# Two layers of cross attention and routed experts on one core: the first column scores drawn forward, loads reordered, one split moved

## The chip, the cores and the metric

The kernel runs on one core of a Trainium2 chip. Five engines work side by side, each on its own list of instructions: TensorE (PE) multiplies matrices, VectorE (DVE), ScalarE (ACT) and GpSimd (POOL) work elementwise, and SyncE (SP) issues DMA transfers and waits. They meet only at semaphores. Times are device microseconds (us) of one launch; smaller is better.

## The reference

Two batches of 256 tokens with 128 features pass through two layers. Each layer is attention over a context of 512 tokens and a mixture of experts, each with its residual. In short:

```python
def _L0_xattn_ref(query, key, value, mask, ...):        # 16 heads of 8 features
    q, k, v = proj(query, w_q, b_q), proj(key, w_k, b_k), proj(value, w_v, b_v)
    scores = einsum('bhqd,bhkd->bhqk', q, k) / sqrt(8)
    scores = where(mask == 0, -1e9, scores)
    attn = softmax(scores, axis=-1)
    return einsum('bhqk,bhkd->bhqd', attn, v) ... @ w_out.T + b_out
x = x + _L0_xattn_ref(_layernorm(x), ctx, ctx, mask, ...)
x = x + _L0_ffn_ref(_layernorm(x), ...)                  # 16 experts, 4 chosen, and a shared one
x = x + _L1_xattn_ref(_layernorm(x), ctx, ctx, ...)      # no mask
x = x + _L1_ffn_ref(_layernorm(x), ...)                  # 8 experts, 2 chosen
```

## The kernel before

All of the kernel's order is written by hand: each engine's function lists its steps, and semaphores tie them together. The change lies in the first attention, and in the first third of the span.

**Projections.** K of a batch is one matmul into a bank. To keep single precision with bfloat16 matmuls, K and Q are split into three bfloat16 parts each. The parts are written to a scratch tensor in HBM and read back in another layout (`k_stack`, `q_stack`), in which the products of the parts lie along the contraction. For K this is `k_out(i)` and `k_in(i, heads, signal)`, for Q `q_out(i)` and `q_in(i, heads, signal)`; i counts layer and batch, so 0 and 1 are the two batches of layer 0. All of these are issued by SP, in one queue. `k_split(i, part)` on GpSimd makes the three parts of K (part 0 takes the rest, part 1 the second part, part 2 the third); only K of batch 0 is split by VectorE and ScalarE. Q is split by VectorE (`q_split`, lines 770 to 775).

**One head.** The attention of a layer runs over 32 heads (16 of each batch), one step s for each, and some steps more for the pipeline to drain. For each head there are, in this order of dependence:
- row scores: `score_rows(n, qt)`, one matmul of 128 queries by 512 keys for each half of the queries (line 342); VectorE adds the mask's bias and takes the maximum of each row (`head_max`, line 791);
- for each pair of heads (group g) GpSimd splits the maxima in three (`max_split`, lines 1459 to 1462), TensorE transposes them (`max_transpose`, line 356) and ScalarE copies them into rows 96 to 98 of `q_stack` (`max_copy`);
- column scores: `score_cols(n, kts)`, the transposed scores with the maximum subtracted by the matmul itself, in two halves, each one bias matmul (line 383) and two of 256 columns (line 387); they need the second mask, turned into a bias by VectorE (`column_bias`);
- the exponential on ScalarE (line 1247), and for four heads together the product with V (`values`, line 410).

**What sets the order.** In step s TensorE issues the row scores of head s and the column scores of head s - 5 (`LAG`), the values lag 9 steps (`PV_LAG`). A head's row scores wait until the maxima of the head before have been read out of the same bank. Row scores of head 0 wait for `first_stacked`, of head 4 for `second_stacked` and `q_stacked[0]`, of head 8 for `k_stacked[0]`, of head 16 for `k_stacked[1]` and `q_stacked[1]`. GpSimd's list `maxima(groups, extra)` runs the extra steps marked g right behind max split g. SP issues the loads in the order of its list, and a wait in it holds up all that follows: the write of batch 1's K waits for its parts (`k_parts[1]`), the write of batch 1's Q for `q_parts[1]`.

Of the kernel before, what the change touches and what calls it, by code (L numbers as in the profile page):

```python
# [23 lines left out]
H, DK = 16, 8  # L24
QT, KT = S // 128, S2 // 128
PARTS = 3
# [16 lines left out]
APART = 32  # L43
LAG = 5
BEGUN = 4
PV_LAG = LAG + HG
HEADS = B * H

# [6 lines left out]
def attention_ffn_kernel(nc, x, ctxT, mask, maskT, attn_w, cols, rows, gate_bias, ties, ident,  # L55
                         gate0, gate1, wg0, wu0, wd0, wsd0, select0, wu1, bu1, wd1, bd1, out):
    ctx = ExitStack()
    with ctx:
# [211 lines left out]
        block = ctx.enter_context(nc.Block())  # L270
        use = {}

        def banks0(b, i):


            if b == 0:
                return (0, 4, 2)[i % 3], i - 3
            return (4, 2)[i % 2], PAIRS0 + i - 2 if i >= 2 else 4 + i
# [3 lines left out]
        def _(pe):  # L282
# [43 lines left out]
            def score_rows(n, qt):  # L326

                l, b, h = n // HEADS, n % HEADS // H, n % H
                if n == 0 and qt == 0:
                    pe.wait_ge(first_stacked, 16 * (PARTS + 1))  # L330
                    pe.wait_ge(k_evacuated, 2)
                if n == HG and qt == 0:
                    pe.wait_ge(second_stacked, 16 * PARTS)
                    pe.wait_ge(q_stacked[0], 16)
                if n == 2 * HG and qt == 0:
                    pe.wait_ge(k_stacked[0], 16 * PARTS)
                if n >= H and h == 0 and qt == 0:
                    pe.wait_ge(k_stacked[l * B + b], 16 * PARTS)
                    pe.wait_ge(q_stacked[l * B + b], 16)
                if n >= 1:  # L340
                    pe.wait_ge(max_done, 2 * (n - 1) + qt + 1)
                mm(bank[:, qt, :], q_stack[0:STACK, b, h, qt * 128:(qt + 1) * 128],  # L342
                   k_stack[0:STACK, b, h, :], start=True, stop=True).then_inc(for_max, 1)
# [225 lines left out]
            def attention(l, extra):  # L569


                for s in range(HEADS + PV_LAG):
                    n, m = l * HEADS + s, l * HEADS + s - LAG
                    if l * BEGUN <= s < HEADS:
                        score_rows(n, 0)
                    if 0 <= s - LAG < HEADS:
                        score_cols(m, range(0, KT // 2))
                    if l * BEGUN <= s < HEADS:
                        score_rows(n, 1)
                    if s % MG == 1 and 0 <= (s - 3) // MG < HEADS // MG:  # L580
                        max_transpose(l * HEADS // MG + (s - 3) // MG)
                    if 0 <= s - LAG < HEADS:
                        score_cols(m, range(KT // 2, KT))
                    if s % HG == (PV_LAG + 1) % HG and s >= PV_LAG + HG:
                        o_transpose(l * B * NG + (s - PV_LAG) // HG - 1)
                    if s >= PV_LAG and (s - PV_LAG) % 2 == 0:
                        values(l * B * NG + (s - PV_LAG) // HG, (s - PV_LAG) % HG // 2)
                    for at, f in extra:
                        if at == s:
                            f()  # L590
# [127 lines left out]
        def _(dve):  # L718
# [342 lines left out]
            def column_bias():  # L1061
                dve.wait_ge(ld["mask_k"], 16)
                ts(bias_k[:, :, :], mask_k[:, :, :], 0.0, MASKED, ALU.is_equal, ALU.mult).then_inc(mask_ready, 1)

            attention(0, [
                (1, lambda: column_bias()),
                (3.5, lambda: norm_stats("a0", 1, x_sb[:, 1])),
                (5.5, lambda: normalise("a0", 1, x_sb[:, 1])),
                (8.5, lambda: xT_copy("a0", 1)),
# [109 lines left out]
        def _(act):  # L1179
# [58 lines left out]
            def exponentials(n):  # L1238
                g = n // HG
                if n == 0:  # L1240

                    act.wait_ge(mask_ready, 2)
                act.wait_ge(scores_ready, n + 1)
                if n >= 2 * HG:
                    act.wait_ge(pv_done, g - 1)
                at = 2 + 2 * (n % 2)
                act.activation(probs[:, n % (2 * HG), :], bank[:, at:at + 2, :].rearrange("p a n -> p (a n)"), ACT.Exp,  # L1247
                               scale=SCALE).then_inc(exp_done, 1)
# [24 lines left out]
            def attention(l, extra):  # L1273
                for s in range(HEADS + PV_LAG):
                    if s % MG == 1 and 0 <= (s - 3) // MG < HEADS // MG:
                        max_copy(l * HEADS // MG + (s - 3) // MG)
                    if 0 <= s - LAG < HEADS:
                        exponentials(l * HEADS + s - LAG)
                    if s % HG == (PV_LAG - 1) % HG and s >= PV_LAG:
                        o_copy(l * B * NG + (s - PV_LAG) // HG)  # L1280
                    for at, f in extra:
                        if at == s:
                            f()
# [111 lines left out]
        def _(pool):  # L1395
# [13 lines left out]
            def add_row(s, b, name):  # L1409
                r = row[:, ROW_NAMES.index(name), :].unsqueeze(1).to_broadcast([128, QT, D])  # L1410
                if s == 0:
                    pool.wait_ge(ld["row"], 16)
                    pool.wait_ge(ld["x"], 16)
                if s == 2:
                    pool.wait_ge(res_ready[2], QT * (b + 1))
                if s == 3:
                    pool.wait_ge(res_ready[3], b + 1)
                pool.tensor_tensor(res_bias[s][b][:, :, :], res[s][b], r, ALU.add).then_inc(res_bias_ready[s], 1)
# [5 lines left out]
            def k_sign(b, heads):  # L1424
                pool.memset(k_stack[MAX_ROW:ROWS_K, b, heads].bitcast(F32), TWO_MINUS_ONES).then_inc(k_signed[b], 1)

            def q_zero(b):
                pool.memset(q_stack[PAD_ROW:MAX_ROW, b].bitcast(F32), 0.0).then_inc(q_zeroed[b], 1)
                pool.wait_ge(q_zeroed[b], 1)
# [13 lines left out]
            def v_bias(i):  # L1443
                l, b = divmod(i, B)
                pool.wait_ge(v_copied[i], 1)
                pool.wait_ge(ld["row"], 16)
                v = v_heads[l][:, b * KT:(b + 1) * KT, :, 0:DK]
                bias = row[:, ROW_NAMES.index(f"bv{l}"), :].rearrange("p (h d) -> p h d", h=H)
                pool.tensor_tensor(v, v, bias.unsqueeze(1).to_broadcast([128, KT, H, DK]), ALU.add)\
                    .then_inc(v_ready[i], 1)  # L1450
# [13 lines left out]
            def k_split(i, part):  # L1464

                if part == 0:
                    pool.wait_ge(k_evacuated, i + 1)
                    pool.tensor_tensor(k_rest[i][:, :], k_full[i][:, :], k_part[i][:, 0, :], ALU.subtract)\
                        .then_inc(k_rest_ready[i], 1)
                elif part == 1:  # L1470
                    pool.wait_ge(k_rest_ready[i], 1)
                    then(pool.tensor_copy(k_part[i][:, 1, :], k_rest[i][:, :]))
                else:
                    pool.tensor_tensor(k_part[i][:, 2, :], k_rest[i][:, :], k_part[i][:, 1, :], ALU.subtract)\
                        .then_inc(k_parts[i], 1)
# [13 lines left out]
            def maxima(groups, extra):  # L1489
# [4 lines left out]
                        if at == g:  # L1494
                            f()

            k_split(1, 0)
            k_split(1, 1)
            k_split(1, 2)
            maxima(range(0, HEADS // MG), [  # L1500
                (0, lambda: v_bias(0)),
                (1, lambda: root("a0", 1)),
                (2, lambda: pool.wait_ge(max_parts, 3)),
                (2, lambda: q_zero(1)),
                (3, lambda: pool.wait_ge(max_parts, 4)),
                (3, lambda: k_sign(1, slice(0, H // 2))),
                (3, lambda: pool.wait_ge(k_signed[1], 1)),
                (4, lambda: pool.wait_ge(max_parts, 5)),
                (4, lambda: k_sign(1, slice(H // 2, H))),
                (4, lambda: pool.wait_ge(k_signed[1], 2)),  # L1510
                (5, lambda: v_bias(1)),
                (6, lambda: add_row(0, 0, "bo0")),
                (7, lambda: v_bias(2)),
                (8, lambda: v_bias(3)),
                (8, lambda: k_split(2, 0)),
# [48 lines left out]
        def _(sp):  # L1564
# [6 lines left out]
            def k_out(i):  # L1571
                sp.wait_ge(k_parts[i], 1)
                sp.dma_start(k_bounce[i][:, :, 0:S2].rearrange("a p s -> p a s"), k_part[i][:, :, :]).then_inc(k_written[i], 16)
# [23 lines left out]
            q_out(0)  # L1597
            k_in(0, slice(0, HG), first_stacked)
            q_in(0, slice(0, HG), first_stacked)
            sp.dma_start(mask_k[:, :, :], maskT.rearrange("(t p) q -> p t q", p=128)).then_inc(ld["mask_k"], 16)  # L1600
            q_in(0, slice(HG, H), q_stacked[0])
            k_in(0, slice(HG, 2 * HG), second_stacked)
            k_in(0, slice(2 * HG, H), k_stacked[0])
            k_out(1)
            k_in(1, every, k_stacked[1])
            sp.dma_start(sel_f[:, :, :], select0).then_inc(ld["sel"], 16)
# [96 lines left out]
```

## Time and profile before

| | |
|---|---|
| three runs | 297.86, 299.78, 302.04 us; median 299.78 |
| profiled execution | 295.13 us, its span 293.2 us |
| TensorE busy | 247.4 us, 84% |
| VectorE | 201.1 us, 69% |
| ScalarE | 149.8 us, 51% |
| GpSimd | 82.0 us, 28% |
| mean granted TensorE clock | 0.941 |

The span runs from the first to the last instruction. A share is the busy time over the span, so it is a mean over stages with different limits. The granted clock is 1.00 at 2.4 GHz and 0.50 at 1.2 GHz. The chain that ended last consists of TensorE for 60%, VectorE 20%, DMA 5%.

### The profile page before, as it was taken

The page shows a single profiled execution, that of the slowest core. Times are in us where ns is not written, and L with a number is a line of the kernel's source. Part 1 is how long each engine was busy: PE and PEld are TensorE (multiplying, and loading weights), DVE is VectorE, ACT ScalarE, POOL GpSimd, SP SyncE. Part 2 cuts the span into 40 slices and gives each one's busy share as a digit, 9 for nine tenths or more (in the row PEclk, how much of TensorE's full clock was granted, in tenths as well). Part 3 has the DMA queues.
Part 4 walks back from the last instruction along what each step waited for, and adds up shares of the span by engine and source line. Part 5 has one row for each costly group of instructions (what it writes and reads, how often), then busy time and mean ns, then how long its engine had stood idle before and what let it go on. Part 6 is the DMA issues. An engine that isn't in the chain of part 4 may idle for free.

```text
span 293.2 us, 5209 instructions
## 1 busy us (share of the span) xinstructions
PE 247.4 (84%) x1701; PEld 141.3 (48%) x1712; DVE 201.1 (69%) x603; ACT 149.8 (51%) x218; POOL 82.0 (28%) x225
## 2 busy tenths in 40 slices
PE   3937989899977996788898898999998889898970
PEld 1611444454443573666576434444444346555670
DVE  5828767766755844597866985767676538888854
ACT  6710466557744743441322454677666535727360
POOL 8504564265522000100300341222213103433321
PEclk9985799999999998999999857999999999999997
DMA  7388597701100068600032630500000000000000
GB/s 235 134 237 180 114 192 273 185 1 57 56 1 0 2 102 128 95 0 0 0 96 69 198 90 0 161 3 1 2 2 0 1 2 1 0 2 0 19 2 18
DMA packets 18406, 19.52 MB, mean 67 GB/s; under 512 B 1996, under 2 KB 16180, under 8 KB 18036
## 3 DMA queue, kind: packets, MB, share of 16 engines
q1 hardware_dynamic: 17804, 18.25, 25.5%
q10 hardware_dynamic: 576, 0.94, 0.9%
q8 instruction: 14, 0.23, 0.3%
q14 instruction: 12, 0.10, 0.1%
HBM read 14.98 MB, written 4.19 MB: 65 GB/s over the span
## 4 chain that ended last, share of the span: by engine, by line
PE 60%; DVE 20%; issue 8%; DMA 5%; ACT 3%; SPq 1%; POOL 1%; DVEq 1%; POOLq 0%; ACTq 0%
PE bank L410 11%; PE bank L342 8%; PE bank L387 8%; PE bank L533 5%; PE bank L564 5%; DVE row_max L794 4%; PE bank L356 4%; PE bank L383 3%; DMA k_stack<-k_bounce 3%; PE bank L498 2%; PE bank L515 2%; PE bank L499 2%; PE bank L549 2%; PE bank L535 2%; DVE early L943 2%
## 5 line engine op out<-in xcount | busy, mean ns | idle before, releaser
L1247 ACT ACTIVATE probs<-bank 128x1024 f32<-128x1024 f32 x64 | 65.4, 1024 | 33.2 <-PE bank L387 28.1
L342 PE MATMUL bank<-k_stack,q_stack 72*128 72x512 bf16 x128 | 53.7, 425 | 10.4 <-DMA q_stack<-q_bounce 4.4
L791 DVE CUSTOM_DVE_ANT_0 discard<-bank,bias_q 128x512 bf16<-128x512 f32 x64 | 42.6, 689 | 26.4 <-PE bank L342 23.6
L387 PE MATMUL bank<-q_stack,k_stack 99*128 99x256 bf16 x256 | 51.6, 287 | 1.3 <-issue 1.0
L794 DVE TENSOR_REDUCE row_max<-bank 128x1 f32<-128x512 f32 x64 | 40.9, 684 | 14.0 <-PE bank L342 13.3
L1233 ACT COPY q_stack<-bank 3x512 bf16<-3x512 bf16 x32 | 18.5, 578 | 36.4 <-PE bank L356 35.7
L410 PE MATMUL bank<-probs,v_ext 128*32 128x256 f32 x512 | 35.1, 393 | 0.8 <-ACT o_sb L1254 0.8
L387 PEld LDWEIGHTS bank<-q_stack,k_stack 99*128 99x128 bf16 x256 | 24.7, 102 | 22.1 <-issue 4.7
L1459 POOL CAST max_part<-row_max 128x4 bf16<-128x4 f32 x32 | 6.6, 207 | 93.1 <-DVE row_max L794 57.2
L342 PEld LDWEIGHTS bank<-k_stack,q_stack 72*128 72x128 bf16 x128 | 12.7, 101 | 33.3 <-DVE row_max L794 9.6
L1329 ACT ACTIVATE early<-bank,col 128x256 f32<-128x256 f32 x32 | 15.5, 563 | 18.7 <-PE bank L549 18.7
L383 PE MATMUL bank<-bias_k,idb 128*128 128x512 bf16 x53 | 20.7, 391 | 0.0
L410 PEld LDWEIGHTS bank<-probs,v_ext 128*32 128x32 f32 x512 | 13.7, 110 | 13.5 <-issue 7.0
L564 PE MATMUL bank<-experts_w,early 128*128 128x128 f32 x128 | 16.3, 281 | 2.5 <-ACT early L1329 2.5
L356 PE MATMUL bank<-idb,max_part 128*3 128x128 bf16 x128 | 13.3, 231 | 6.0 <-DVEq L760 2.1
L533 PE MATMUL bank<-experts_w,xT_f 128*128 128x512 f32 x32 | 17.4, 625 | 0.0
L564 PEld LDWEIGHTS bank<-experts_w,early 128*128 128x128 f32 x128 | 14.9, 192 | 4.0 <-DVE shared_area L996 3.1
L498 PE MATMUL bank<-xT_f,experts_w 128*128 128x256 f32 (+1 forms) x52 | 16.4, 397 | 0.0
L499 PE MATMUL bank<-xT_f,experts_w 128*128 128x256 f32 (+1 forms) x52 | 15.5, 379 | 0.0
L356 PEld LDWEIGHTS bank<-idb,max_part 128*3 128x3 bf16 x128 | 7.2, 86 | 16.2 <-issue 16.2
L515 PE MATMUL bank<-experts_w,early 128*128 128x128 f32 x96 | 13.7, 292 | 1.5 <-DVE early L945 1.4
L1305 ACT ACTIVATE early<-bank 128x512 f32<-128x512 f32 x12 | 7.2, 598 | 14.6 <-PE bank L499 14.3
(179 smaller groups left out, 380.2 us busy)
## 6 DMA issues: line engine op xcount, KB each, us to landing
k_stack<-k_bounce SPq DMA_DIRECT2D x9, 384.0 KB
q_bounce<-q_part SPq DMA_DIRECT2D x12, 192.0 KB, 2.4
q_stack<-q_bounce SPq DMA_DIRECT2D x3, 576.0 KB
k_bounce<-early SPq DMA_DIRECT2D x4, 384.0 KB, 2.6
experts_w<-in_wu SPq DMA_DIRECT2D x1, 1024.0 KB, 5.1
experts_w<-in_wg SPq DMA_DIRECT2D x1, 816.0 KB, 9.4
experts_w<-in_wu SPq DMA_DIRECT2D x1, 816.0 KB, 10.9
experts_w<-in_wd SPq DMA_DIRECT2D x1, 768.0 KB, 7.2
```

Source lines behind the costliest of these rows:

```text
L342: mm(bank[:, qt, :], q_stack[0:STACK, b, h, qt * 128:(qt + 1) * 128], k_stack[0:STACK, b, h, :], start=True, stop=True).then_inc(for_max, 1)
L356: last = pe.transpose(o[:, at:at + 128], max_part[:, g % 2, j, t, :], idb[:, :])
L383: mm(bank[:, at + kts[0] // 2, :], idb[:, :], bias_k[:, kts[0]:kts[0] + 2, :].rearrange("p t q -> p (t q)"), start=True, stop=False)
L387: last = mm(o, k_stack[:, b, h, kt * 128:(kt + 1) * 128], q_stack[:, b, h, :], start=(l == 1), stop=(l == 1 or kt == kts[-1]))
L410: last = mm(bank[VW * j:VW * (j + 1), OUT, 0:S], v_ext[l][:, b * KT + kt, h * (DK + 1):h * (DK + 1) + VW], probs[:, (g * HG + j) % (2 * HG ...
L498: mm(bank[0:m, at + j, 0:S], wg0_sb[:, t * 128:t * 128 + m], xT["f0"][b][:, :], start=True, stop=True)
L499: last = mm(bank[0:m, at + j, S:2 * S], wu0_sb[:, t * 128:t * 128 + m], xT["f0"][b][:, :], start=True, stop=True)
L533: mm(o, xT["f1"][b][:, t * 128:(t + 1) * 128], wu1_sb[:, 2 * i:2 * i + 2, :].rearrange("p e n -> p (e n)"), start=True, stop=False)
L564: last = mm(bank[:, OUT, (e * QT + t) * D:(e * QT + t + 1) * D], hid1[:, w % 2, 2 * e + half, t * 128:(t + 1) * 128], wd1_sb[:, 2 * (2 * i ...
L791: ins = dve.tensor_tensor_reduce(discard[:, qt, :], bank[:, qt, :], bias_q[:, qt, :], 1.0, LOWEST, ALU.add, ALU.max, o)
L794: ins = dve.tensor_reduce(o, bank[:, qt, :], AX.X, ALU.max)
L1247: act.activation(probs[:, n % (2 * HG), :], bank[:, at:at + 2, :].rearrange("p a n -> p (a n)"), ACT.Exp, scale=SCALE).then_inc(exp_done, 1)
```

## The change

Four edits in one. Column scores of heads 0, 1, 2 and 3 of layer 0 are issued 3, 3, 4 and 4 steps behind the row scores, in steps 3, 4, 6 and 7, instead of 5 steps behind, in steps 5 to 8; the others stay at 5, so steps 5 and 8 have none. In step 3 the transposes of the first maxima go ahead of the column scores that need them. ScalarE's exponentials follow the same steps. VectorE's column bias moves from behind head 1's maxima to behind head 2's. K and Q of heads 4 to 7 are loaded ahead of the second mask, the Q load of heads 4 to 15 becomes two, of 4 to 7 and of 8 to 15. On GpSimd the split of batch 1's K, which stood ahead of all maxima, goes behind max splits 2 and 3, and the steps that stood there go one to two groups later.

```diff
+FIRST_LAGS = (3, 3, 4, 4)
...
+        def column_step(l, m):
+            return m + (FIRST_LAGS[m] if l == 0 and m < len(FIRST_LAGS) else LAG)
+        head_of_step = [{column_step(l, m): m for m in range(HEADS)} for l in range(2)]
...
                 if n == HG and qt == 0:
-                    pe.wait_ge(second_stacked, 16 * PARTS)
-                    pe.wait_ge(q_stacked[0], 16)
+                    pe.wait_ge(second_stacked, 16 * (PARTS + 1))
                 if n == 2 * HG and qt == 0:
                     pe.wait_ge(k_stacked[0], 16 * PARTS)
+                    pe.wait_ge(q_stacked[0], 16)
...
+                    transposes = s % MG == 1 and 0 <= (s - 3) // MG < HEADS // MG
+                    at_once = columns and m == n - MG - 1
                     if l * BEGUN <= s < HEADS:
                         score_rows(n, 0)
-                    if 0 <= s - LAG < HEADS:
+                    if transposes and at_once:
+                        max_transpose(l * HEADS // MG + (s - 3) // MG)
+                    if columns:
                         score_cols(m, range(0, KT // 2))
                     if l * BEGUN <= s < HEADS:
                         score_rows(n, 1)
-                    if s % MG == 1 and 0 <= (s - 3) // MG < HEADS // MG:
+                    if transposes and not at_once:
                         max_transpose(l * HEADS // MG + (s - 3) // MG)
-                    if 0 <= s - LAG < HEADS:
+                    if columns:
                         score_cols(m, range(KT // 2, KT))
...
-                (1, lambda: column_bias()),
+                (2, lambda: column_bias()),
...
-            k_split(1, 0)
-            k_split(1, 1)
-            k_split(1, 2)
             maxima(range(0, HEADS // MG), [
-                (0, lambda: v_bias(0)),
                 (1, lambda: root("a0", 1)),
-                (2, lambda: pool.wait_ge(max_parts, 3)),
-                (2, lambda: q_zero(1)),
-                (3, lambda: pool.wait_ge(max_parts, 4)),
-                (3, lambda: k_sign(1, slice(0, H // 2))),
-                (3, lambda: pool.wait_ge(k_signed[1], 1)),
+                (2, lambda: k_split(1, 0)),
+                (2, lambda: v_bias(0)),
+                (3, lambda: k_split(1, 1)),
+                (3, lambda: k_split(1, 2)),
                 (4, lambda: pool.wait_ge(max_parts, 5)),
-                (4, lambda: k_sign(1, slice(H // 2, H))),
-                (4, lambda: pool.wait_ge(k_signed[1], 2)),
-                (5, lambda: v_bias(1)),
-                (6, lambda: add_row(0, 0, "bo0")),
+                (4, lambda: q_zero(1)),
+                (5, lambda: pool.wait_ge(max_parts, 6)),
+                (5, lambda: k_sign(1, slice(0, H // 2))),
+                (5, lambda: pool.wait_ge(k_signed[1], 1)),
+                (6, lambda: pool.wait_ge(max_parts, 7)),
+                (6, lambda: k_sign(1, slice(H // 2, H))),
+                (6, lambda: pool.wait_ge(k_signed[1], 2)),
+                (7, lambda: v_bias(1)),
+                (8, lambda: add_row(0, 0, "bo0")),
...
             k_in(0, slice(0, HG), first_stacked)
             q_in(0, slice(0, HG), first_stacked)
+            k_in(0, slice(HG, 2 * HG), second_stacked)
+            q_in(0, slice(HG, 2 * HG), second_stacked)
             sp.dma_start(mask_k[:, :, :], ...)
-            q_in(0, slice(HG, H), q_stacked[0])
-            k_in(0, slice(HG, 2 * HG), second_stacked)
             k_in(0, slice(2 * HG, H), k_stacked[0])
+            q_in(0, slice(2 * HG, H), q_stacked[0])
             k_out(1)
             k_in(1, every, k_stacked[1])
```

## Rows read from the trace of the kernel before

**Rows 1.** Busy us by stretch; behind them granted clock, DMA share, GB/s.
```profile
20.00:21.00 1.00, 0.78 (x2) 0.13 (x2) 0.14 (x1) 0.00 (x0) 0.00 (x0) 0.50 1.02 352
31.00:32.00 1.00, 1.00 (x5) 0.58 (x5) 0.29 (x2) 0.58 (x1) 0.50 (x3) 0.50 0.03 8
33.00:34.00 1.00, 1.00 (x7) 0.58 (x6) 1.00 (x4) 0.16 (x1) 1.00 (x1) 0.90 0.65 173
57.00:80.00 23.00, 22.59 (x193) 11.31 (x196) 15.54 (x51) 16.26 (x21) 12.56 (x33) 1.00 0.12 39
```

**Rows 2.** Instructions in time, TensorE: start, us, operation [idle before <-releaser].
```profile
20.22 1.03 PE L342 MATMUL bank<-k_stack,q_stack 72*128 72x512 bf16 x2 [4.37 <-DMA q_stack<-q_bounce]
...
27.26 1.03 PE L342 MATMUL bank<-k_stack,q_stack 72*128 72x512 bf16 x2 [0.68 <-DMA k_stack<-k_bounce]
...
29.93 0.62 PE L342 MATMUL bank<-k_stack,q_stack 72*128 72x512 bf16 x1
...
55.63 0.38 PE L342 MATMUL bank<-k_stack,q_stack 72*128 72x512 bf16 x1 [0.72 <-issue]
```

**Rows 3.** The same view, transfers issued by SP.
```profile
17.97 0.40 SPq L1600 DMA_DIRECT2D probs<-in_maskT  x1
...
22.08 0.50 SPq L1573 DMA_DIRECT2D k_bounce<-early  x1
31.26 2.56 SPq L1580 DMA_DIRECT2D k_stack<-k_bounce  x3
...
37.70 0.47 SPq L1614 DMA_DIRECT2D experts_w<-in_wu  x1
45.17 1.49 SPq L1586 DMA_DIRECT2D q_bounce<-q_part  x3
50.19 0.32 SPq L1592 DMA_DIRECT2D q_stack<-q_bounce  x1
```

**Rows 4.** The same view, GpSimd.
```profile
11.85 1.16 POOL L1468 TENSOR_TENSOR early<-early 128x512 f32<-128x512 f32 x1 [3.03 <-ACT early L1186]
13.07 0.61 POOL L1472 CAST early<-early 128x512 bf16<-128x512 f32 x1
13.76 1.21 POOL L1474 TENSOR_TENSOR early<-early 128x512 bf16<-128x512 f32 x1
...
25.01 1.19 POOL L1449 TENSOR_TENSOR v_ext<-v_ext,row 128x512 f32<-128x512 f32 x1
...
31.36 0.20 POOL L1459 CAST max_part<-row_max 128x4 bf16<-128x4 f32 x1 [0.94 <-DVE row_max L791]
...
32.17 0.21 POOL L1462 TENSOR_TENSOR max_part<-max_rest,max_part 128x4 bf16<-128x4 f32 x1
```

**Rows 5.** The same view, VectorE.
```profile
12.22 0.93 DVE L774 CAST q_part<-q_rest 128x256 bf16<-128x256 f32 x1
13.19 0.77 DVE L775 TENSOR_TENSOR q_part<-q_rest,q_part 128x256 bf16<-128x256 f32 x1
...
30.59 0.69 DVE L791 CUSTOM_DVE_ANT_0 discard<-bank,bias_q 128x512 bf16<-128x512 f32 x1
...
44.39 0.29 DVE L774 CAST q_part<-q_rest 128x256 bf16<-128x256 f32 x1
44.72 0.43 DVE L775 TENSOR_TENSOR q_part<-q_rest,q_part 128x256 bf16<-128x256 f32 x1
```

**Rows 6.** Time from issue to landing of transfers; the first line is the K writes' (L1573).
```profile
DMA to landing us min/median/max: 2.6/2.6/9.2
...
probs<-in_maskT SPq DMA_DIRECT2D x1, 512.0 KB, 4.8
...
experts_w<-in_wu SPq DMA_DIRECT2D x1, 816.0 KB, 10.9
...
q_bounce<-q_part SPq DMA_DIRECT2D x12, 192.0 KB, 2.4
```

**Rows 7.** The chain of waits that ended last: start, us, what.
```profile
31.61 0.43 PE bank L387 x2
```

More of the change, by code:

```diff
@@ L572, in attention @@
                 for s in range(HEADS + PV_LAG):
-                    n, m = l * HEADS + s, l * HEADS + s - LAG
+                    n, columns = l * HEADS + s, s in head_of_step[l]
+                    m = l * HEADS + head_of_step[l].get(s, 0)
+                    transposes = s % MG == 1 and 0 <= (s - 3) // MG < HEADS // MG
+                    at_once = columns and m == n - MG - 1
                     if l * BEGUN <= s < HEADS:
                         score_rows(n, 0)
-                    if 0 <= s - LAG < HEADS:
+                    if transposes and at_once:
+                        max_transpose(l * HEADS // MG + (s - 3) // MG)
+                    if columns:
                         score_cols(m, range(0, KT // 2))
@@ L1276, in attention @@
                         max_copy(l * HEADS // MG + (s - 3) // MG)
-                    if 0 <= s - LAG < HEADS:
-                        exponentials(l * HEADS + s - LAG)
+                    if s in head_of_step[l]:
+                        exponentials(l * HEADS + head_of_step[l][s])
                     if s % HG == (PV_LAG - 1) % HG and s >= PV_LAG:
```

## The prediction

> **What bounds the kernel now.** The page comes first: its TensorE share (in the table above) is the highest of all engines. The busy time by stretch then says where this change can act. From 57 to 80 us TensorE is busy 22.59 of 23.00 us at full clock [rows 1], so in the steady part of the first attention nothing is won or lost unless TensorE's work changes, and it doesn't. Before that there are holes: the engine starts the heads at 20.22 after 4.37 us without work, its granted clock is then 0.50 (1.2 GHz), and it climbs to 0.90 only in the slice 33 to 34 us, after work without a hole since 29.93 [rows 1, 2]. In between it was busy 1.00 of 1 us at 0.50. The TensorE timeline shows two later waits for loads: head 4's rows at 27.26 behind K, 0.68 us, and head 16's rows (batch 1's first head) at 55.63, after 0.72 us. Two rows matmuls per head and the order of issue say that 55.63 is head 16. It is the step that needs batch 1's K and Q in SBUF; batch 1's Q load was issued at 50.19 [rows 3], so its landing, about 5.2 us later, is what ends that wait. So batch 1's loads are already the latest thing at head 16. The last view is SP's own queue, which is where the change does most.
>
> **The parts, and what each costs.**
>
> 1. *GpSimd no longer splits batch 1's K at the start.* Before, the three splits run from 11.85 to 14.97 [rows 4], beside VectorE's last two steps of batch 0's Q split: cast 0.93 and subtract 0.77, against 0.29 and 0.43 for the same two steps at 44.39, with GpSimd idle [rows 5]. These feed the Q write that the first head waits for. Gain: 0.64 + 0.34 = 1.0 us at the first head (20.2 to 19.2). The Trainium skill ("SBUF — State Buffer", section "Who interferes with whom") says that a VectorE cast in a 2-port mode, or a VectorE operation with two SBUF inputs beside a reading GpSimd operation, excludes GpSimd and the other way round; the rows agree. The same rule speaks for no slowdown where the splits go now, because the head maxima read only one operand from SBUF.
>
> 2. *Second quarter's loads ahead of the second mask.* In SP's order 288 KB of K and 144 KB of Q (from the shapes) now stand before the mask. Before, 432 + 288 = 720 KB lay between the mask's landing (17.97 + 4.8 = 22.8) and the K that released head 4 at 27.2, which is 6.1 ns a KB [rows 2, 3, 6]. So the mask lands 432 KB later and, with everything issued 1.0 earlier, at 22.8 + 2.6 - 1.0 = 24.4. Heads 4 to 7 have landed by about 22 and never wait. The bias from the mask, moved behind head 2's maxima, is ready at about 25.1. The price of the 0.68 us wait at head 4 goes to the column scores of head 0, which could start no earlier anyway, since they want the first max copy at about 25.0.
>
> 3. *Column scores of heads 0 to 3 at lags 3, 3, 4, 4.* They fill TensorE from 25.3 on. At low clock a half of the column scores takes twice the 0.43 us of two 256-column matmuls, 0.86 (the bias matmul has as many columns as those two), and a rows matmul, again 512 columns, 0.43 [rows 7]. From 25.3: columns 0 and rows 3, then columns 1 and rows 4, reach 30.1; the clock, by what the engine did before 33 (3.2 us without a hole), has risen by then. Heads 5, 6, 7 follow at full clock, paced by VectorE's 0.69 a maximum [rows 5], the statistics and the normalising of batch 1. That puts head 5's last maximum at about 31.8 and head 7's at about 35.0. By head 9 both orders are the same. TensorE arrives at head 16 some 3 us earlier than before, at 51 to 52. If head 16's data were there, this would be the gain, 3 us.
>
> 4. *Batch 1's K split between later maxima.* This is the step that decides. On GpSimd, after head 5: one max split of 1.02 (31.36 to 32.38), first K split 1.16, V bias 1.19, max split 1.02, then the two other K splits, 0.61 and 1.21, and gaps of some 0.07 between them [rows 4]: 6.4 us. From 31.8 this ends at 38.2; head 7's maxima at 35.0 don't hold it. Before, the parts were ready at 14.97.
>
> SP waits for these parts ahead of everything that follows in its queue: the write of batch 1's K, its load (three transfers of 384 KB), the selection matrix, router constants, both expert weights of 816 KB, and then batch 1's Q write and load. Before, the K write was issued at 22.08 but landed only 9.2 us later, behind the loads in the queue, and the load was issued at 31.26 [rows 3, 6]. In 38.2 + 2.6 (the quickest landing of such a write) = 40.8 the load goes out 9.5 us later than before. The queue will be idle meanwhile: before, batch 0 was in and the queue quiet (0.03 busy) already at 31 to 32 us [rows 1].
>
> From the K load on, the queue is worked off without a gap. The second expert weight was issued at 37.70 and landed 10.9 us later, at 48.6; batch 1's Q write, issued at 45.17 with its parts ready, was not done until 50.19 though the median of such transfers is 2.4 us: it stood behind the weights [rows 3, 6]. So the time from K load to the end of the Q write, 18.9 us, is the queue's, and moves as a whole by 9.5. Q is then written at 59.7, loaded by 64.9, and head 16's rows go at 55.63 + 9.5 = 65.1. The V biases, sign and zero memsets that move on GpSimd go to later head pairs; I cost them at nothing. They are covered by at least 13 us of waiting at head 16; the heaviest later group (row bias 0.7, V bias 1.2, K split 1.2, max split 1.0) is 4.1 us against about 4.2 us for two heads, so even without cover it would cost some tenths.
>
> The Trainium skill ("DMA: Bandwidth & Descriptors", section "Queues, rings and completion order") states that on each DMA engine the descriptors of a ring are consumed in order while completions may not be first in, first out. If only the loose half held here, the Q load wouldn't have to wait for the weights, and the sum would end at no change (rival C).
>
> 5. *The clock after the stall.* TensorE stands still from about 51.5 to 65. After the 4.37 us hole before 20.22 it was at 0.50, and work without a hole from 29.93 to about 33.1 passed before it was back [rows 1, 2]. Half of 3.2 us is lost: 1.6. Bounds: nothing (if the clock is granted at once), and 3.2 (if it takes twice as long).
>
> The stall isn't made good later: only 0.41 of 23 us is free on TensorE between 57 and 80 [rows 1].
>
> **Sum.** The gains of parts 1 to 3 vanish into the wait at head 16. + 9.5 (K load later, whole queue) + 1.6 (clock) = + 11.1 us. The span of 293.2 becomes 304.3, the profiled execution's 295.13 us becomes 306.2. That execution is 4.65 below the median of the runs, 299.78; on the median it is 310.9, which I give as the time. Bounds of the K parts: earliest, heads 0 to 5 entirely at VectorE's pace from 19.2 (0.64 for the first rows matmul, 12 x 0.62 between maxima, bias 0.6, statistics 0.7) end at 28.6, + 6.4 = 35.0, shift 6.3; latest, head 5's maxima two us after mine, 40.2, shift 11.5. With 0 to 1.6 for the clock (3.2 at the outside) that is + 6.3 to + 13.1.
>
> **Rivals.**
>
> A. *The forecast*: head 16 waits for batch 1's Q to about 65; chance 0.64; 308 to 314.
>
> B. *Smaller stall*: the early columns bring the clock and the maxima forward enough that the K parts are ready at about 35 to 36, or the queue regains some, having fewer transfers beside it; no clock loss. + 6.3 to + 8: 306 to 308. For it: VectorE has idle time in this stretch. Against: the max split of heads 6 and 7 stands behind 2.4 us of GpSimd work. Chance 0.17.
>
> C. *The other side, not slower*: the queue doesn't hold batch 1's Q behind the weights. Place: the Q write behind the weights. SP reaches the Q write at 38.17 + 9.5 = 47.7; issued over 1.5 us and landed in 2.6 it is written at 51.5, and the load lands 4 to 5 us later at about 56: head 16 goes within 0.5 us of before, 300 to 301. It decides if the Q load lands before about 57. Against: the 5 us of the Q write before, where 2.4 is usual. Chance 0.12.
>
> D. *A gain*: batch 1's loads don't matter and the 3 us of part 3 remain, 296 to 297. It would need the Q load to land by 52, while the Q write can't be issued before 47.7. Chance 0.03; over 2% faster is less still, and I give 0.02.
>
> E. *Worse*: the clock stays low for longer, or the queue runs slower beside other work: over 314. Chance 0.04.
>
> **Range and chances.** A 2% difference (6 us) is about what a measurement of this kernel can tell from no change. Slower by over 2%: A, E and most of B, 0.82. Within 2%: C, the rest of B, most of D, 0.16. Faster: 0.02. The range 304.5 to 314.5 takes A and B and leaves C, D, E outside; its lower end also holds the bounds' low end if the runs come out a little below the median of before, as the profiled one did.
>
> **What would show it.** In the trace after: first rows matmul at about 19.2, and the casts of batch 0's Q at about 0.3 and 0.4; batch 0's second mask landing near 24.4; K parts of batch 1 near 38, SP's wait on GpSimd there some 15 us long; K load issued near 41; DMA share near zero between 30 and 38; a TensorE idle time of 12 to 14 us in front of a rows matmul, released by the Q load, near 65; granted clock at half for some 3 us behind it. Wrong would be: a Q write done within 3 us of issue while the weights are still under way, a K load issued before 37, or TensorE catching up behind the stall.

## The result, and the profile after

The changed kernel is slower: 310.62 us median (308.53 to 313.30, 4 runs) against 300.91 (297.86 to 302.30, 4 runs) for the kernel before; the ratio is 1.0405, 95% interval 1.0345 to 1.0465. The prediction said 310.9 us, 304.5 to 314.5, slower by over 2% with 0.82. The profiled execution took 313.30 us with a span of 311.5, above its kernel's median; the one of before, 295.13, was below its own. Some executions of a kernel come out over 1.5% above its fastest: the ratios and their intervals leave these out, the medians keep them, and the profiled executions of the changed kernel and of kernels 3 and 7 below are such ones. So the traces differ by more (18.3 us of span) than the medians (9.7), and what is read from them is checked below on kernel 2, which has the same stall and a profiled execution of 311.72 us beside a median of 310.56.

From the page of the changed kernel: the totals, the granted clock in 40 slices, and the group of rows matmuls with the idle time in front of it.

```profile
span 311.5 us, 5211 instructions
...
PE 250.9 (81%) x1701; PEld 142.9 (46%) x1712; DVE 198.7 (64%) x603; ACT 149.6 (48%) x218; POOL 81.1 (26%) x225
...
PEclk9985999755999999979999985799999999999997
...
L349 PE MATMUL bank<-k_stack,q_stack 72*128 72x512 bf16 x128 | 54.1, 428 | 22.9 <-issue 16.0
```

The work is the same, 1701 matmuls in both; TensorE is busy for 250.9 us in place of 247.4, at a mean granted clock of 0.918 in place of 0.941. What is new is idle time in front of row scores, 16.0 us of it put down to no engine, and a dip of the clock in slices 9 and 10. The TensorE timeline of the changed kernel (start, us, operation, idle before) shows where:

```profile
20.59 0.61 PE L349 MATMUL bank<-k_stack,q_stack 72*128 72x512 bf16 x2 [3.92 <-DMA q_stack<-q_bounce]
...
27.94 0.64 PE L394 MATMUL bank<-q_stack,k_stack 99*128 99x256 bf16 x2 [2.24 <-DVE bias_k L1075]
...
53.95 1.07 PE L417 MATMUL bank<-probs,v_ext 128*32 128x256 f32 x16
69.74 0.58 PE L349 MATMUL bank<-k_stack,q_stack 72*128 72x512 bf16 x1 [14.72 <-issue]
...
79.62 0.38 PE L427 MATMUL bank<-idf,o_sb 128*128 128x128 f32 x2
```

Head 16's rows go at 69.74 where they went at 55.63 [rows 2], after 14.72 us of nothing. The engine arrived there at 55.02, no earlier than before (54.91). The same kernel's transfers on SP's queue, and SP's wait ahead of the K write of batch 1:

```profile
19.44 0.40 SPq L1614 DMA_DIRECT2D probs<-in_maskT  x1
...
39.68 0.38 SPq L1585 DMA_DIRECT2D k_bounce<-early  x1
43.82 2.54 SPq L1592 DMA_DIRECT2D k_stack<-k_bounce  x3
...
49.85 0.44 SPq L1627 DMA_DIRECT2D experts_w<-in_wu  x1
50.33 4.29 SPq L1598 DMA_DIRECT2D q_bounce<-q_part  x3
64.25 0.32 SPq L1604 DMA_DIRECT2D q_stack<-q_bounce  x1
```
```profile
SPq L1585 <- POOL early L1486: 17.9, 1, 17.9
```

Against [rows 3]: the K write of batch 1 goes out at 39.68 and not at 22.08, its load at 43.82 and not at 31.26, the Q load at 64.25 and not at 50.19. SP stood 17.9 us before GpSimd's third part. GpSimd's timeline gives the reason:

```profile
33.63 0.19 POOL L1471 CAST max_part<-row_max 128x4 bf16<-128x4 f32 x1 [0.81 <-DVE row_max L803]
...
34.59 1.18 POOL L1480 TENSOR_TENSOR early<-early 128x512 f32<-128x512 f32 x1
35.73 1.20 POOL L1461 TENSOR_TENSOR v_ext<-v_ext,row 128x512 f32<-128x512 f32 x1
36.87 0.19 POOL L1471 CAST max_part<-row_max 128x4 bf16<-128x4 f32 x1
...
37.81 0.61 POOL L1484 CAST early<-early 128x512 bf16<-128x512 f32 x1
38.50 1.15 POOL L1486 TENSOR_TENSOR early<-early 128x512 bf16<-128x512 f32 x1
```

From head 5's maxima (33.63) to the third part (39.65) it is the row of work that the prediction added up, 6.0 us against 6.4, only begun 1.8 us later. Stretches of the changed kernel (busy us of TensorE, weight loads, VectorE, ScalarE, GpSimd, then clock, DMA share, GB/s):

```profile
31.00:39.00 8.00, 6.98 (x40) 3.16 (x38) 7.59 (x29) 4.22 (x5) 5.79 (x14) 0.97 0.00 1
55.00:69.70 14.70, 0.02 (x3) 0.00 (x0) 0.00 (x0) 0.29 (x1) 2.98 (x6) 0.63 0.78 222
69.70:79.10 9.40, 9.14 (x40) 3.67 (x42) 3.50 (x10) 2.89 (x4) 3.73 (x7) 0.50 0.20 50
```

The first line shows both halves of the story: the DMA engines do nothing for eight microseconds (0.00), because everything behind the K write in SP's list waits with it, and VectorE is full (7.59 of 8). The second is the stall: TensorE and VectorE stand idle, and the DMA engines work off the queue (0.78). The third is the clock: 9.4 us at half rate although TensorE is busy for 9.14 of them.

VectorE of the changed kernel:

```profile
12.92 0.29 DVE L786 CAST q_part<-q_rest 128x256 bf16<-128x256 f32 x1
13.25 0.43 DVE L787 TENSOR_TENSOR q_part<-q_rest,q_part 128x256 bf16<-128x256 f32 x1
...
26.61 0.69 DVE L1075 TENSOR_SCALAR bias_k<-probs 128x1024 bf16<-128x1024 int32 x1 [1.48 <-DMA probs<-in_maskT]
...
29.04 0.69 DVE L803 CUSTOM_DVE_ANT_0 discard<-bank,bias_q 128x512 bf16<-128x512 f32 x1 [1.12 <-PE bank L349]
```

The casts of Q are as short as said, against [rows 5]. The last line is the second maximum of head 3. The fixed point used below is the second time that TensorE transposes the output of four heads, 79.62 in the timeline above. In the kernel before these two were

```profile
26.11 0.69 DVE L791 CUSTOM_DVE_ANT_0 discard<-bank,bias_q 128x512 bf16<-128x512 f32 x1
...
61.09 0.38 PE L420 MATMUL bank<-idf,o_sb 128*128 128x128 f32 x2
```

### The profile page after: what moved, and what is told of

The parts are those of the page before. It is cut to its first block, busy times and chain, and to the rows that moved or that the text cites. A ratio compares the mean times of both kernels' runs of the same rounds, so it can differ in the third digit from the quotient of the medians.

```text
span 311.5 us, 5211 instructions
## 1 busy us (share of the span) xinstructions
PE 250.9 (81%) x1701; PEld 142.9 (46%) x1712; DVE 198.7 (64%) x603; ACT 149.6 (48%) x218; POOL 81.1 (26%) x225
## 4 chain that ended last, share of the span: by engine, by line
PE 54%; DVE 18%; issue 12%; DMA 9%; POOL 3%; SPq 1%; ACT 1%; DVEq 0%; POOLq 0%; ACTq 0%
PE bank L417 9%; PE bank L349 7%; PE bank L394 7%; PE bank L540 5%; PE bank L571 4%; DVE row_max L806 4%; DMA k_stack<-k_bounce 3%; PE bank L363 3%; PE bank L390 3%; PE bank L522 2%; PE bank L505 2%; DMA probs<-in_maskT 2%; PE bank L506 2%; PE bank L556 2%; PE bank L542 2%
## 5 line engine op out<-in xcount | busy, mean ns | idle before, releaser
L394 PE MATMUL bank<-q_stack,k_stack 99*128 99x256 bf16 x256 | 52.9, 293 | 3.5 <-DVE bias_k L1075 2.2
L806 DVE TENSOR_REDUCE row_max<-bank 128x1 f32<-128x512 f32 x64 | 40.9, 683 | 14.0 <-PE bank L349 13.3
L417 PE MATMUL bank<-probs,v_ext 128*32 128x256 f32 x512 | 36.0, 401 | 0.8 <-ACT o_sb L1266 0.8
L390 PE MATMUL bank<-bias_k,idb 128*128 128x512 bf16 x53 | 21.8, 412 | 0.4 <-ACT q_stack L1245 0.3
L571 PEld LDWEIGHTS bank<-experts_w,early 128*128 128x128 f32 x128 | 14.9, 192 | 4.0 <-DVE shared_area L1008 3.1
L522 PEld LDWEIGHTS bank<-experts_w,early 128*128 128x128 f32 x96 | 13.0, 206 | 3.2 <-DVE early L957 2.2
```

The costliest lines, as they stand in the source:

```text
L390: mm(bank[:, at + kts[0] // 2, :], idb[:, :], bias_k[:, kts[0]:kts[0] + 2, :].rearrange("p t q -> p (t q)"), start=True, stop=False)
L394: last = mm(o, k_stack[:, b, h, kt * 128:(kt + 1) * 128], q_stack[:, b, h, :], start=(l == 1), stop=(l == 1 or kt == kts[-1]))
L417: last = mm(bank[VW * j:VW * (j + 1), OUT, 0:S], v_ext[l][:, b * KT + kt, h * (DK + 1):h * (DK + 1) + VW], probs[:, (g * HG + j) % (2 * HG ...
L522: last = mm(bank[:, OUT, t * D:(t + 1) * D], hid0[0:m, u % 2, j, t * 128:(t + 1) * 128], w, start=(i == 0 and j == 0 and t == 0), stop=sha ...
L571: last = mm(bank[:, OUT, (e * QT + t) * D:(e * QT + t + 1) * D], hid1[:, w % 2, 2 * e + half, t * 128:(t + 1) * 128], wd1_sb[:, 2 * (2 * i ...
L806: ins = dve.tensor_reduce(o, bank[:, qt, :], AX.X, ALU.max)
```

## The experiments

Twelve kernels, each beside runs of the kernel before on the same chip. Ratios are to the kernel before.

| kernel | median us | ratio, 95% interval |
|---|---|---|
| changed kernel | 310.62 | 1.0405 (1.0345 to 1.0465) |
| 1 split put back | 301.42 | 1.0126 (1.0046 to 1.0206) |
| 2 split alone | 310.56 | 1.0427 (1.0367 to 1.0488) |
| 3 Q ahead of weights | 303.58 | 1.0160 (1.0069 to 1.0251) |
| 4 weights ahead of K | 302.73 | 1.0157 (1.0091 to 1.0223) |
| 5 filled stall, 68 | 309.41 | 1.0356 (1.0286 to 1.0426) |
| 6 loads alone | 297.59 | 0.9993 (0.9958 to 1.0029) |
| 7 lags alone | 301.17 | 0.9980 (0.9920 to 1.0041) |
| 8 split behind Q | 300.75 | 1.0007 (0.9959 to 1.0055) |
| 9 filled stall, 52 | 310.19 | 1.0265 (1.0162 to 1.0368) |
| 10 filled start | 299.70 | 1.0014 (0.9972 to 1.0056) |
| 11 lags, filled start | 295.21 | 0.9862 (0.9798 to 0.9926) |
| 12 split behind Q and Q ahead | 295.89 | 0.9900 (0.9866 to 0.9934) |

The kernel before had medians of 299.10, 298.36 and 299.33 in the three groups of runs (1 to 4, 5 to 8, 9 to 12). In kernels 7 and 9 the ratio and the median point apart.

**1 and 2: which part costs.** The changed kernel with only GpSimd's split put back, and the kernel before with only GpSimd's new list.

```diff
# 1, from the changed kernel
+            k_split(1, 0)
+            k_split(1, 1)
+            k_split(1, 2)
             maxima(range(0, HEADS // MG), [
...
-                (2, lambda: k_split(1, 0)),
...
-                (3, lambda: k_split(1, 1)),
-                (3, lambda: k_split(1, 2)),
# 2, from the kernel before: the changed kernel's whole list of maxima(...), nothing else
```

> The changed kernel with one part undone: GpSimd splits batch 1's K ahead of all maxima again. Lags, load order and the rest of GpSimd's list stay changed. Theory (the split alone costs the time): batch 1's K parts are ready near 15, the load goes out near 31, head 16's rows run at 55 to 56 without a stall, and the time is that of the kernel before, 297 to 302 us. Rival (the later mask and the early column scores cost time themselves): head 16 is reached later than 56.5 and the time is over 304. Rival (the early columns pay once their data is there): under 296.

> The kernel before with GpSimd's list of the changed kernel and nothing else. Theory: K parts of batch 1 near 38 to 40, K load issued 42 to 44, TensorE idle 12 to 15 us ahead of head 16's rows, time 309 to 313 us, as the changed kernel. Rival (the stall needs the new loads or lags too): under 304.

Kernel 2 alone is as slow as the whole change (1.0427 beside 1.0405); kernel 1 is 1.3% above before (0.5 to 2.1). Rows of kernel 2, TensorE and then SP:

```profile
68.46 0.58 PE L342 MATMUL bank<-k_stack,q_stack 72*128 72x512 bf16 x1 [13.15 <-issue]
...
76.42 0.38 PE L420 MATMUL bank<-idf,o_sb 128*128 128x128 f32 x2
```
```profile
39.15 0.38 SPq L1573 DMA_DIRECT2D k_bounce<-early  x1
41.74 2.51 SPq L1580 DMA_DIRECT2D k_stack<-k_bounce  x3
...
62.66 0.32 SPq L1592 DMA_DIRECT2D q_stack<-q_bounce  x1
```

The stall of 13.15 us is there with the old loads and the old lags, so GpSimd's list causes it by itself; and since kernel 1 keeps the rest of that list moved and has no stall, it is the split's place. Kernel 1's time is inside its forecast, but its head 16 is not: it goes without a wait at 61.02, not at 55 to 56. That and its 1.3% are told under 6 to 8.

**3 and 4: is it the queue behind the K load?** Kernel 3 takes the changed kernel and puts the Q write and load of batch 1 right behind the K load; kernel 4 leaves them and puts the weights ahead of the K write, where SP would otherwise only wait.

```diff
# 3
             k_in(1, every, k_stacked[1])
+            q_out(1)
+            q_in(1, every, q_stacked[1])
             sp.dma_start(sel_f[:, :, :], select0).then_inc(ld["sel"], 16)
...
# 4: sel_f, g0_sb, g1_sb, gbias, tie_f, bu1_sb, wg0_sb, wu0_sb issued ahead of
             k_out(1)
```

> The changed kernel with one edit in SP's order: batch 1's Q write and load go right behind batch 1's K load, ahead of the selection matrix, the router constants and the two expert weights. The K parts come as late as in the changed kernel (near 39.7). Theory (the Q load stood behind 2.1 MB of other loads in one queue): Q written near 55, loaded near 60, head 16's rows near 60.5 in place of 69.7, time 300 to 304 us. Rival (the queue doesn't hold the Q write back, its late landing has another cause): head 16 stays at 68 to 70, time 309 to 313.

> The changed kernel with the selection matrix, router constants and the two expert weights issued ahead of batch 1's K write, so that they fill the queue while SP waits for GpSimd. Nothing else changes. Theory: the idle stretch between 25 and 39 us is used, K load still near 43.8, Q write right behind it, head 16's rows near 60, time 300 to 304 us. Rival (the wait for the K parts is what counts, not the queue behind it): head 16 at 68 to 70, time 309 to 313.

Kernel 3's SP rows and its head 16, then kernel 4's:

```profile
43.06 2.51 SPq L1592 DMA_DIRECT2D k_stack<-k_bounce  x3
...
56.36 0.33 SPq L1604 DMA_DIRECT2D q_stack<-q_bounce  x1
```
```profile
63.27 0.58 PE L349 MATMUL bank<-k_stack,q_stack 72*128 72x512 bf16 x1 [9.39 <-issue]
```
```profile
42.59 2.51 SPq L1592 DMA_DIRECT2D k_stack<-k_bounce  x3
...
54.65 0.32 SPq L1604 DMA_DIRECT2D q_stack<-q_bounce  x1
```
```profile
60.10 0.59 PE L349 MATMUL bank<-k_stack,q_stack 72*128 72x512 bf16 x1 [6.77 <-issue]
```

K parts and K load are late as in the changed kernel (the load goes out 0.8 and 1.2 us earlier), but without 2.1 MB of weights between them and Q the Q load goes out 13.3 and 12.1 us behind the K load and not 20.4, head 16 goes 6.5 and 9.6 us earlier, and both kernels are within their forecast time. The queue theory holds, its rival (head 16 at 68 to 70) is out. In kernel 3 head 16 came at 63.27 and not near 60.5: its Q load took 6.9 us from issue to the rows with the other loads issued right behind it, against 5.5 in kernel 4 and 5.4 before. The stall that remains, 9.39 and 6.77 us, is put down to the late K parts, as kernel 1 has none.

**5 and 9: what the clock costs behind the stall.** TensorE is kept busy through the stall by matmuls whose result head 16 overwrites.

```diff
+                if n == H and qt == 0:
+                    pe.wait_ge(max_done, 2 * (n - 1) + 1)
+                    for _ in range(WARM):      # 68 in kernel 5, 52 in kernel 9
+                        mm(bank[:, 0, :], idb[:, :], bias_k[:, 0:2, :]..., start=True, stop=True)
```

> The changed kernel with 68 matmuls of 512 columns on TensorE between head 15's and head 16's work, whose result is overwritten; they fill about 14.7 us at 0.216 each, which is the time the engine stands idle there. Nothing else changes. Theory (the stall also costs clock: 1.6 us in the prediction, and about 4 by the profile of the changed kernel, where the engine ran at 0.50 from 69.7 to 79.1): the clock stays at 1.00 through 70 to 80 us and the time falls by 3 to 4.5 us to 306 to 307.5. Rival (the low clock behind the stall costs little, other engines set the pace there): 309 to 312, and the same spacing of heads 16 to 19 as in the changed kernel.

> The changed kernel with 52 overwritten matmuls ahead of head 16, in place of the 68 of the run before: those ended at 68.82, by the transfers' times some 2 to 3 us behind the landing of Q, and so held head 16 back themselves. 52 end near 65.5. Theory (the clock behind the stall costs 3.5 to 4.5 us): head 16 goes when Q lands, clock at 1.00 behind it, 305 to 307.5 us. Rival (it costs no more than the 1.6 of the prediction or nothing): 308.5 to 311.

TensorE of kernel 5, then of kernel 9:

```profile
54.13 14.85 PE L348 MATMUL bank<-bias_k,idb 128*128 128x512 bf16 x67
68.82 0.38 PE L354 MATMUL bank<-k_stack,q_stack 72*128 72x512 bf16 x1
```
```profile
53.22 11.40 PE L348 MATMUL bank<-bias_k,idb 128*128 128x512 bf16 x52
66.08 0.38 PE L354 MATMUL bank<-k_stack,q_stack 72*128 72x512 bf16 x1 [1.47 <-issue]
...
71.55 0.38 PE L432 MATMUL bank<-idf,o_sb 128*128 128x128 f32 x2
```

In kernel 9 head 16 waits 1.47 us more for Q behind the fillers, and from its rows to the next output transposes it takes 5.47 us, the 5.46 of before (55.63 to 61.09). Without fillers the same stretch takes 9.88 in the changed kernel, 7.96 in kernel 2, 9.20 in kernel 3 and 7.30 in kernel 4. So the clock costs 4.4, 2.5, 3.7 and 1.8 us there: real, and different in each execution. The two larger figures are of profiled executions of 313.30 us (median 310.62) and 308.63 us (median 303.58), the two smaller of 311.72 (median 310.56) and 301.08 (median 302.73). Kernel 5's 68 fillers ran on to 68.8 and held the heads back themselves, my mistake in the count, and its time, 309.41, missed the forecast of 306 to 307.5. In the time of whole runs the gain isn't settled: kernel 9's two quickest runs, on which its ratio rests, are 305.19 (inside the forecast) and 307.72 (just outside), but its six runs reach 312.86, their median of 310.19 is in the rival's range, and the intervals of kernel 9 and the changed kernel meet.

**6, 7 and 8: the other parts.** Loads alone on the kernel before; lags alone with the column bias at 2; and the changed kernel with the split put back but behind a wait.

```diff
# 8, from kernel 1
+            pool.wait_ge(q_parts[0], 1)
             k_split(1, 0)
```

> The kernel before with the new order of loads alone (heads 4 to 7 ahead of the second mask), lags and GpSimd's list as before. VectorE's column bias stands behind head 1's maxima here, so its wait for the mask holds up head 2's maxima. Theory (the late mask is what costs 1% beside the split): the mask lands near 26.5, VectorE waits about 3 us there, time 301 to 304 us. Rival (the lags cost, the mask doesn't): within 0.5% of before.

> The kernel before with the new lags (3, 3, 4, 4) and the column bias behind head 2's maxima, but the old order of loads and GpSimd's old list. Theory (columns start earlier, TensorE is better filled, nothing is late): at most 3 us won, 295 to 299.5 us. Rival (early columns delay the row scores, hence the maxima, and gain nothing): within 0.5% of before or up to 1% slower.

> The changed kernel with the K split of batch 1 ahead of all maxima again, but behind a wait for batch 0's Q parts, so that it runs at about 13.6 to 16.7 us and not beside VectorE's last two steps of the Q split (0.93 and 0.77 us beside the split, 0.29 and 0.43 without it). Theory: parts near 16.7, K write issued near 22 as before, first rows matmul some 1.0 us earlier than with the split at the old place, time 1 us under that of the kernel with the split put back (301.4), 299.5 to 301. Rival (what starts the heads is not the Q parts): the same as with the split put back.

By their ratios all three are the same as before. In kernel 6 the mask comes late, at 27.80 and not near 26.5, and VectorE waits 3.42 us for it ahead of head 2's maxima:

```profile
27.80 0.69 DVE L1063 TENSOR_SCALAR bias_k<-probs 128x1024 bf16<-128x1024 int32 x1 [3.42 <-DMA probs<-in_maskT]
```

and the time doesn't move: the theory that the late mask costs 1% fell. Kernel 7's forecast of up to 3 us gained isn't borne out either (ratio 0.998). Over all their runs kernels 7 and 8, which have the new lags, have medians of 301.17 and 300.75 beside 298.36 for the kernel before and 297.59 for kernel 6. 8 and 6 of their 12 runs are above 300.9 us, against 4 of 29 before and none of 12 of kernel 6. So whether the lags cost something stays open. Kernels 1 and 8 differ by the place of the split alone. VectorE of kernel 1 has the long casts again:

```profile
12.62 1.07 DVE L786 CAST q_part<-q_rest 128x256 bf16<-128x256 f32 x1
13.72 0.77 DVE L787 TENSOR_TENSOR q_part<-q_rest,q_part 128x256 bf16<-128x256 f32 x1
```

Its first rows matmul is at 21.21, kernel 8's at 19.71: 1.5 us. Their ratios, 1.0126 and 1.0007, point the same way, with intervals that just meet; the 1.5 us would be less than half of the 3.6 us between them. The rest wasn't tested. In the traces kernel 1's clock is back to 1.00 at 48 us and kernel 8's by 42.

Kernels 1 and 7 also show how the clock behaves in a stretch without a stall. One line of each, in this order, and a longer stretch of kernel 1:

```profile
36.00:40.00 4.00, 4.00 (x16) 1.64 (x14) 3.02 (x7) 1.48 (x2) 1.12 (x2) 0.50 1.01 138
```
```profile
36.00:40.00 4.00, 4.00 (x16) 1.71 (x14) 2.19 (x8) 2.16 (x3) 1.51 (x6) 0.50 1.08 126
```
```profile
30.00:47.00 17.00, 16.45 (x67) 6.60 (x66) 10.69 (x33) 6.86 (x8) 6.69 (x20) 0.50 0.80 160
```

From 36 to 40 us TensorE is busy without a break and still at half clock, when the profiled execution of before had been back to full clock since 34 us. In kernel 1 that lasts until 48 us, and in kernels 6, 8 and 10 the clock comes back between 40 and 42. Head 16's rows go at 61.02 in kernel 1, 59.60 in kernel 6, 59.39 in kernel 8 and 60.29 in kernel 10, against 55.63 in the profiled execution of before. Kernels 6, 8 and 10 time as before, so that execution was a quick one in just this stretch.

**10, 11 and 12: what could be faster.** Kernel 10 keeps TensorE busy with overwritten matmuls from 16 to 20 us and in heads 0 to 2. Kernel 12 is the kernel before with two small edits. Kernel 11 joins the two edits, the new lags and the fillers.

```diff
# 12, from the kernel before
+            pool.wait_ge(q_parts[0], 1)
             k_split(1, 0)
...
             k_in(1, every, k_stacked[1])
+            q_out(1)
+            q_in(1, every, q_stacked[1])
             sp.dma_start(sel_f[:, :, :], select0).then_inc(ld["sel"], 16)
# 10, from the kernel before
             v_projection(3, 3)
+            pe.wait_ge(k_evacuated, 3)
+            pe.wait_ge(consts_ready, 1)
+            filler(FIRST)            # FIRST = 17
...
+                if n < 3:
+                    filler(1 + qt)       # at the end of score_rows
```

> The kernel before with 17 overwritten matmuls of 512 columns on TensorE between the projections and head 0, and three more with each of the heads 0 to 2, so that the engine is not idle from 15.9 to 20.2. Nothing else. Theory (half clock from 20 to 33 us, in some executions for longer, costs time in the first heads): the clock stays at 1.00 up to head 4 at least, 1 to 4 us faster, 294 to 297.5 us. Rival (VectorE's maxima and the loads set the pace of the first heads, the clock doesn't): the same as before.

> The kernel before with two small edits: the K split of batch 1 waits for batch 0's Q parts, and batch 1's Q write and load go ahead of the weights. Lags, loads and the rest as before. Theory: head 0 about 1.0 us earlier, head 16 without its 0.7 us wait, together 1 to 1.7 us faster, 296.5 to 297.5 beside 298.4. Rival (head 4's wait for K takes the gain back): the same as before within 0.3%.

> The new lags with the old order of loads, batch 1's K split ahead of the maxima but behind batch 0's Q parts, batch 1's Q write and load ahead of the weights, and the same overwritten matmuls. Theory: the parts of the change that are not the late split gain what the clock allows, 1 us by the earlier Q parts, 0.7 by the Q load at head 16, 1 to 4 by the clock: 292 to 296 us. Rival (TensorE's clock falls anyway at the wait for the mask, and the early columns delay the maxima): 296 to 300.

Kernel 10 is the same as before. Two of its stretches:

```profile
25.00:30.00 5.00, 2.48 (x12) 0.67 (x12) 3.70 (x12) 0.58 (x1) 3.08 (x9) 1.00 0.85 152
...
34.00:36.00 2.00, 2.00 (x8) 1.04 (x7) 2.00 (x5) 0.53 (x2) 1.54 (x1) 0.50 0.49 121
```

The clock is at 1.00 where TensorE has only 2.5 of 5 us of work, and has fallen when the work comes, with engine and VectorE both full. Full clock was bought at the wrong time, and the forecast (up to 4 us faster) missed.

Kernels 11 and 12 beat both kernels: 0.9862 (0.9798 to 0.9926) and 0.9900 (0.9866 to 0.9934). Kernel 11's median is inside its forecast of 292 to 296, kernel 12's 0.6 us below its own. Kernel 12's head 16:

```profile
54.97 0.38 PE L342 MATMUL bank<-k_stack,q_stack 72*128 72x512 bf16 x1 [0.58 <-issue]
```

That is 0.66 us earlier than in the profiled execution of before; the rest of its 1% (3 us) isn't found by its trace. Its 12 runs lie within 294.26 to 296.74, those of before beside it within 296.65 to 303.25, so part of the gain may be that its executions all come out as quick as the profiled one of before (295.13); why was not tested, nor which of its two edits gains.

## Why the prediction was right, step by step

The direction, the cause and the place were right: kernel 2 has the whole loss, kernels 3 and 4 take most of it back by the queue alone, and head 16 is where TensorE stands. That the time agrees to 0.3 us is in part luck, since terms cancel. On traces, as microseconds later than the kernel before:

| term | predicted | changed kernel | kernel 2 |
|---|---|---|---|
| K load issued | 9.5 | 12.6 | 10.5 |
| K load to Q load, Q load to rows | 0 | 1.5 | 2.4 |
| clock behind the stall | 1.6 | 4.4 | 2.5 |
| rest of the kernel | 0 | -0.2 | 1.4 |
| span | 11.1 | 18.3 | 16.7 |

- *Q parts (part 1).* The steps took 0.29 and 0.43 as said. But in this execution the first of them began 0.7 us later than before, behind a later Q projection, so the first head went at 20.59, not 19.2. Kernels 1 and 8 show 1.5 us for the same edit.
- *Mask (part 2).* Forecast for 24.4, and 26.6 in the trace: 7.15 us from issue to landing. Too low by 2.2, without effect on the end.
- *The 3 us to be had without the stall (part 3).* This step was wrong. TensorE arrived at head 16 at 55.02, against 54.91 before, and kernels 7 and 8 gain nothing in time. In kernels 3, 4 and 9, with the same lags and loads, it arrived at 53.88, 53.33 and 53.22, so 1.0 to 1.7 of the 3 us were there. In the changed kernel the second half of head 3's row scores stands behind head 0's columns, which stand behind the mask, so head 3's second maximum came at 29.04 in place of 26.11. From there VectorE is full, 7.59 of 8 us, and what the columns had won the maxima had lost; this reading is of the one trace. The pieces that the prediction names from 25.3 on (four halves of columns at 0.86, four rows matmuls at 0.43) also add up to 30.5, not 30.1. None of it had weight in the sum, since the stall swallows any gain ahead of it.
- *K parts (part 4).* 39.65 against 38.2, within the bounds of 35.0 to 40.2; the chain on GpSimd was right, head 5's maxima later, for the reason above. The landing of the K write, 2.6 in kernel 2, was 4.1 in the changed kernel.
- *The queue.* It was taken to shift as a whole. It did, and was 1.5 to 2.4 us slower on top. In-order consumption of the ring (by the Trainium skill, "DMA: Bandwidth & Descriptors", section "Queues, rings and completion order") agrees with kernels 3 and 4, where 2.1 MB less in between brought the Q load 7 to 8 us closer to the K load. Rival C is out (the parts that it names put its Q write at 51.8, not 51.5, which changes nothing in it).
- *The clock.* 1.6 predicted, with 3.2 at the outside. Kernels 2 and 4 show 2.5 and 1.8; the changed kernel and kernel 3 show more, 4.4 and 3.7, in the executions of 313.30 and 308.63 us. The 3.2 us of half clock came from the one trace of before, and kernel 1 held half clock for over 17 us, so the term was low and its bound not safe.
- *The base.* Adding to the median of before was a step with a flaw that happened to help. A stall at a fixed time swallows whatever TensorE's clock did ahead of it. The profiled execution of before was quick in its first heads (second output transposes at 61.09; kernels 6, 8 and 10, which time as before, have theirs at 65.08, 64.86 and 65.75, and spans longer by 3.7, 3.5 and 4.9). A usual execution of before already holds some 4 us that the changed kernel loses in the stall. That would bring the 16.7 of kernel 2's trace to the 12.6 that its ratio gives (0.0427 times 296); it is argued from these rows and not shown, since no second profile of the kernel before exists.

## What to carry to other kernels

Work that moves on one engine is priced at the queue it releases: here 3 us of GpSimd work, which cost GpSimd itself no time, held 4 MB of transfers behind a single wait in SP's list, and left the DMA engines empty for some 10 us (share 0.04 or less from 30.0 to 39.7). Before a producer is moved, look for what stands behind its consumer in the queue, and put what doesn't depend on it ahead; experiments 3 and 4 recovered some six tenths of the loss by order alone (ratios 1.0160 and 1.0157 in place of 1.0405). And a gain ahead of a fixed later arrival, here TensorE's head start, is worth nothing until that arrival moves.

## What the runs showed of the hardware that was not expected

- TensorE's clock stays at half rate for very different times under the same full load: back by 34 us after some 3 us of work without a hole in the kernel before, but still 0.50 from 28 to 34 us in kernel 12 (busy for 6.00 of 6.00) and from 30 to 47 us in kernel 1 (busy for 16.45 of 17.00). Behind the stall it was 0.50 for some 5 us in kernel 2 and for 9.4 us in the changed kernel.
- Batch 1's K write, into an idle queue, landed after 2.6 us in kernels 2, 5 and 9, and after 4.1 to 4.6 in the changed kernel and kernels 3 and 4. What decides it stayed open.
- The issue of the three Q writes took 1.5 us in the kernel before, 7.5 us behind that of the second weight [rows 3], and 4.3 us in the changed kernel and 4.7 in kernel 2, right behind it.
